# Router items moved in a layer-1 schedule, rows of their own for the last expert but one, and deviations of seven batches taken before the last residual

## What is computed

```
xn    = LN(x)                              # rows of x, over 128 channels
ao    = differential_attention(xn)         # per batch: softmax(q1 k1) - lam * softmax(q2 k2), 512 keys, times v, RMS norm
h     = LN1(xn); a = group_attention(h)    # over positions in a group, 16 heads
hid   = xn + a @ proj
r     = LN2(hid)                           # the rows that are routed
probs = softmax(r @ router)                # 8 experts, the best two per row, their weights made to sum to 1
for each expert e: out_e = gelu(rows_e @ w1_e) @ w2_e * weight     # up to 1280 rows each
moe   = scatter-add of out_e to the rows they came from
result = x + ao + hid + moe
```

## Time and profile before

| what | us |
|---|---|
| median of 3 runs (lowest, highest) | 1095.08 (1094.47, 1097.09) |
| the profiled execution | 1089.94 |
| its span | 1088.2 |
| PE busy | 921.2 (85%) |
| DVE busy | 712.0 (65%) |
| ACT busy | 624.8 (57%) |
| POOL busy | 567.9 (52%) |

### The profile page before, as it was taken

The page is one execution under the profiler, slowest core; times in us unless marked ns, Lnnn a source line. Parts: engine busy times, 40 slices in busy tenths (PEclk is TensorE's granted clock), DMA queues, the critical chain, the costliest instruction groups (busy, mean ns, idle before and its releaser), DMA issues.

```text
span 1088.2 us, 20697 instructions
## 1 busy us (share of the span) xinstructions
PE 921.2 (85%) x6587; PEld 616.8 (57%) x6624; DVE 712.0 (65%) x1511; ACT 624.8 (57%) x1127; POOL 567.9 (52%) x643
## 2 busy tenths in 40 slices
PE   7688879988999899899999868677888886999890
PEld 4366654477555455555555445444555655998880
DVE  6788852125777677677766565999857773646356
ACT  6566654512878687687878646344578653333320
POOL 3300029270675576566742217998306771788772
PEclk9899989999999999999999969988899997999995
DMA  5011121343101011101101059500011102222229
GB/s 144 1 78 77 77 79 58 136 139 123 31 21 31 19 23 24 28 20 28 24 21 30 2 92 188 178 1 0 6 34 43 50 26 80 83 78 90 75 75 269
DMA packets 75567, 70.23 MB, mean 65 GB/s; under 512 B 6706, under 2 KB 68604, under 8 KB 73440
## 3 DMA queue, kind: packets, MB, share of 16 engines
q1 hardware_dynamic: 65120, 59.84, 20.0%
q0 software_dynamic: 4608, 6.64, 1.8%
q10 hardware_dynamic: 5760, 2.70, 0.9%
HBM read 32.04 MB, written 31.60 MB: 58 GB/s over the span
## 4 chain that ended last, share of the span: by engine, by line
PE 33%; DVE 17%; POOL 9%; issue 9%; ACT 2%; DMA 2%; SPq 1%; DVEq 0%; ACTq 0%; POOLq 0%
PE banks L1984 6%; PE banks L1956 5%; PE banks L1970 5%; POOL y_dram L975 4%; PE banks L2010 4%; DVE B_mneg L1150 2%; PE banks L1958 2%; PE banks L2119 2%; DVE D_dmx L1256 2%; PE banks L2023 2%; PE banks L2068 1%; DVE banks L1305 1%; DVE D_sc L1282 1%; POOL rows_dram L930 1%; SPq L729 1%
## 5 line engine op out<-in xcount | busy, mean ns | idle before, releaser
L1150 DVE TENSOR_REDUCE B_mneg<-banks 128x2 f32<-128x256 f32 (+3 forms) x256 | 208.5, 824 | 78.1 <-PE banks L1958 69.5
L1623 ACT ACTIVATE B_pt<-banks 128x1024 f32<-128x1024 f32 (+3 forms) x256 | 178.7, 708 | 73.9 <-PE banks L1970 68.9
L791 POOL TENSOR_SCALAR_AFFINE_SELECT B_pt<-B_pt 128x512 f32<-128x512 f32 x128 | 81.2, 635 | 171.6 <-ACT B_pt L1623 162.5
L1956 PE MATMUL banks<-B_kp,B_qt 128*128 128x128 bf16 (+3 forms) x507 | 124.9, 300 | 1.8 <-DVE B_mneg L1150 0.6
L1970 PE MATMUL banks<-B_qt,B_kp 128*128 128x256 bf16 (+3 forms) x480 | 105.4, 297 | 12.0 <-issue 5.1
L1958 PE MATMUL banks<-B_mask_q,B_identb 128*128 128x128 bf16 x512 | 102.0, 219 | 0.7 <-issue 0.6
L1772 ACT ACTIVATE F_gh<-banks 128x512 f32<-128x512 f32 (+1 forms) x96 | 50.0, 527 | 82.8 <-PE banks L2188 78.3
L1984 PE MATMUL banks<-B_pt,B_vp 128*32 128x512 f32 (+3 forms) x1024 | 95.9, 446 | 1.5 <-ACT B_ot L1629 0.7
L930 POOL DMA_INDIRECT rows_dram<-F_xs,F_rowi x64 | 62.5, 976 | 61.7 <-DVE F_xs L1343 42.8
L975 POOL DMA_INDIRECT y_dram<-F_yo,F_ide x70 | 70.9, 1012 | 41.7 <-issue 19.2
L2119 PE MATMUL banks<-D_qk 128*128 128x512 f32 x128 | 75.2, 673 | 11.6 <-DVE D_pr L1267 11.6
(11 more groups left out here) (288 smaller groups left out, 2182.4 us busy)
## 6 DMA issues: line engine op xcount, KB each, us to landing
comb_dram<-C_comb SPq DMA_DIRECT2D x8, 1024.0 KB, 3.9
C_cst<-comb_dram SPq DMA_DIRECT2D x8, 1024.0 KB, 4.8
B_kp<-B_kt SPq DMA_DIRECT2D x64, 128.0 KB, 2.4
rows_dram<-D_zeros SPq DMA_DIRECT2D x8, 650.0 KB, 15.0
F_xe<-rows_dram SPq DMA_DIRECT2D x8, 650.0 KB, 3.9
C_w<-w_in SPq DMA_DIRECT2D x16, 256.0 KB, 2.9
y_dram<-D_zeros SPq DMA_DIRECT2D x2, 2048.0 KB, 16.8
F_gw<-mw_in SPq DMA_DIRECT2D x16, 256.0 KB, 3.0
```

The source lines that it names most:

```text
L791: g.affine_select(out=w, in_=w, compare_op=ALU.is_ge, fill=0.0, base=0, pattern=[[0, G], [1, P]], channel_multiplier=-1).then_inc(B_md, 1)
L1150: v.tensor_reduce(mneg[:, g % 2, qt, 2 * hp:2 * hp + 2], banks2[pair_of_banks(item)][:, :, 0:(qt + 1) * P], X, ALU.max, negate=True).then_ ...
L1623: a.activation(pt[:, 2 * hp:2 * hp + 2, PT_AT[kt]:PT_AT[kt] + w], banks2[pair_of_banks(item)][:, :, 0:w], ACT.Exp).then_inc(B_ex, 1)
L1956: t_.matmul(dst, qt1[:, g % 2, hp, qt * P:(qt + 1) * P], kp[:, g % NG, hp, h, 0:(qt + 1) * P], start=True, stop=False)
```

## The change

Three parts.

1. **Router table.** S gets the time 144.7 instead of 152.7. The pairs start at 147.3 + 18.0h instead of 155.3 + 14.1h: 147.3, 165.3, 183.3 and 201.3 instead of 155.3, 169.4, 183.5 and 197.6. All router items move with their pair.
2. **Deviations.** The deviations of the first seven batches are taken before the residual of the last batch, those of the last batch between the first three `norm_rows`. ACT's four roots stand ahead of its wait for the end of layer 0, and ahead of its first copy of turned rows.
3. **The tail.** Expert 6 gets rows of its own, `y_last_but_one`, as expert 7 has `y_last`: one more zero fill of 2 MB, and the two folding instructions for expert 6 too. SP loads `y_dram` when experts 0 to 5 have been scattered, then `y_last_but_one` in 4 pieces. The last iteration of the expert loop is written out on PE and DVE, without the items of a next pair. In it DVE adds `y_dram` for five batches before expert 7's first `yo`, and for three after its last. `y_last` is loaded into the place of `od`, without waiting for adds.

The diff, without the renamed semaphores, the new place of `rst2` and `var2`, and the arguments of the PE round:

```diff
--- before.py
+++ after.py
@@ -305,9 +305,9 @@
         yield t0 + 30.7, ("h", k, 0)
-    yield 152.7, ("S", 0, 0)
+    yield 144.7, ("S", 0, 0)
     for h in range(B // 2):
-        t0 = 155.3 + 14.1 * h
+        t0 = 147.3 + 18.0 * h
         for q in (2 * h, 2 * h + 1):
...
@@ -684,8 +685,9 @@
                              zeros[:, 0:D].unsqueeze(1).broadcast_to([P, TILES, D])).then_inc(D_z, 16)
-            sp.dma_start(y_last[:, :].rearrange("(p n) d -> p n d", p=P),
-                         zeros[:, 0:D].unsqueeze(1).broadcast_to([P, TILES, D])).then_inc(D_z, 16)
+            for k in range(2):
+                sp.dma_start(y_late[k][:, :].rearrange("(p n) d -> p n d", p=P),
+                             zeros[:, 0:D].unsqueeze(1).broadcast_to([P, TILES, D])).then_inc(D_z, 16)
@@ -717,17 +719,16 @@
-            sp.wait_ge(G_x[0], 16 * (EXP // 2))
-            sp.sem_inc(G_x[0], 16)
-            sp.wait_ge(G_w[0], 32 * (EXP // 2))
-            sp.sem_inc(G_w[0], 32)
-
             for par in range(2):
-                sp.wait_ge(G_zs[par], 16 * CT * (EXP // 2 - par))
+                sp.wait_ge(G_zs[par], 16 * CT * (EXP // 2 - 1))
             for b in range(B):
                 for k in range(2):
                     sp.dma_start(xs[:, b, k, :, 0:D], y_dram[(k * B + b) * T:(k * B + b + 1) * T, :].rearrange(
-                        "(t p) d -> p t d", p=P)).then_inc(G_bk[b], 16)
+                        "(t p) d -> p t d", p=P)).then_inc(G_bk[b // 2], 16)
+            sp.wait_ge(G_zs[0], 16 * CT * (EXP // 2))
+            for c in range(B // 2):
+                sp.dma_start(y[:, 2 * c * NT:(2 * c + 2) * NT, :], y_late[0][2 * c * T:(2 * c + 2) * T, :].rearrange(
+                    "(t p) d -> p t d", p=P)).then_inc(G_bs[c], 16)
             for b in range(B):
@@ -864,7 +865,6 @@
-            pool.wait_ge(D_sd, 1)
             own.link(g.memset(zeros[:], 0.0))
...
@@ -932,7 +932,7 @@
-            pool.wait_ge(D_sd, 2)
+            pool.wait_ge(D_sd, 4)
             for kind, a_, n in D_PLAN.order:
@@ -965,16 +965,16 @@
                 pool.wait_ge(G_id, e + 1)
-                last = e == EXP - 1
-                if last:
+                late = e - (EXP - 2)
+                if late >= 0:
                     own.link(g.tensor_scalar(second[:], ide[:, par, :], B * T, B * T, ALU.is_ge, ALU.mult))
                     own.link(g.tensor_tensor(ide[:, par, :], ide[:, par, :], second[:], ALU.subtract))
                 for c, (n0, n) in enumerate(CHUNKS):
                     pool.wait_ge(G_ys, G_ROUNDS.passed("y", pr, False, "y", par, c))
                     for m in range(n0, n0 + n):
                         pool.indirect_dma_start(
-                            out=(y_last if last else y_dram)[:, :], out_offset=bass.IndirectOffsetOnAxis(ap=ide[:, par, m:m + 1], axis=0),
-                            in_=yo[:, par, m, :], in_offset=None, bounds_check=(1 if last else 2) * B * T - 1, oob_is_err=False
+                            out=(y_late[late] if late >= 0 else y_dram)[:, :], out_offset=bass.IndirectOffsetOnAxis(ap=ide[:, par, m:m + 1], axis=0),
+                            in_=yo[:, par, m, :], in_offset=None, bounds_check=(1 if late >= 0 else 2) * B * T - 1, oob_is_err=False
                         ).then_inc(G_zs[par], 16)
@@ -1171,12 +1171,14 @@
-                def residual(g):
+                def residual(g, stats=True):
                     dve.wait_ge(B_mf, B_ROUNDS.passed("misc", it, False, "W", g, 0))
                     dve.wait_ge(B_bo, at(it, g // NG, 1, 1))
                     xb = x[:, bass.ds(it * (2 * NT) + (g // NG) * NT, NT), :].rearrange("p t d -> p (t d)")
                     own.link(v.tensor_tensor(xb, bank[6][:], xb, ALU.add))
                     dve.sem_inc(B_me, 1)
+                    if not stats:
+                        return
@@ -1202,8 +1204,30 @@
                         normalise(g)
+                    elif kind == "W" and last and g == PG - 1:
+                        deviations_of(FIRST_BATCHES, 1)
+                        residual(g, stats=False)
                     elif kind == "W":
                         residual(g)
+
+
+            FIRST_BATCHES, LAST_BATCH = slice(0, TILES - NT), slice(TILES - NT, TILES)
+
+            def variances_of(tiles):
+                v.tensor_copy(sd[:, tiles], st[:, tiles, 1]).then_inc(D_var, 1)
+
+            def deviations_of(tiles, n):
+                if tiles == FIRST_BATCHES:
+                    variances_of(tiles)
+                dve.wait_ge(D_sd, n)
+                own.link(v.reciprocal(rstd[:, tiles], sd[:, tiles]))
+                own.link(v.tensor_tensor(var2[:, tiles], rstd[:, tiles], rstd[:, tiles], ALU.mult))
+                v.tensor_tensor(var2[:, tiles], var2[:, tiles], st[:, tiles, 1], ALU.mult).then_inc(D_var, 1)
+
+            def second_deviations_of(tiles, n):
+                dve.wait_ge(D_sd, n)
+                own.link(v.reciprocal(rst2[:, tiles], var2[:, tiles]))
+
             dve_round(-1, True)
@@ -1213,15 +1237,17 @@
-            v.tensor_copy(sd[:], st[:, 0:TILES, 1]).then_inc(D_var, 1)
-            dve.wait_ge(D_sd, 1)
-            own.link(v.reciprocal(rstd[:], sd[:]))
             dve.wait_ge(B_end, 5)
-
-            own.link(v.tensor_tensor(var2[:], rstd[:], rstd[:], ALU.mult))
-            v.tensor_tensor(var2[:], var2[:], st[:, 0:TILES, 1], ALU.mult).then_inc(D_var, 1)
-            dve.wait_ge(D_sd, 2)
-            own.link(v.reciprocal(rst2[:], var2[:]))
+            second_deviations_of(FIRST_BATCHES, 2)
+
+            def last_batch_stats():
+                for t in range(NT):
+                    ins = v.bn_stats(bn6[:, t, :], x[:, TILES - NT + t, :])
+                own.link(ins)
+                for t in range(NT):
+                    ins = v.bn_aggr(st[:, TILES - NT + t, :], bn6[:, t, :])
+                own.link(ins)
+                variances_of(LAST_BATCH)
@@ -1397,6 +1423,12 @@
                     norm_rows(a_)
+                    if a_ == 0:
+                        last_batch_stats()
+                    elif a_ == 1:
+                        deviations_of(LAST_BATCH, 3)
+                    elif a_ == 2:
+                        second_deviations_of(LAST_BATCH, 4)
                 elif kind == "lam" and a_ != 1:
@@ -1432,11 +1464,22 @@
-            def dve_round_g(it, first):
+            def rows_of(b):
+                return slice(b * NT, (b + 1) * NT)
+
+            def add_earlier(b):
+
+                dve.wait_ge(G_bk[b // 2], 64)
+                own.link(v.tensor_tensor(x[:, rows_of(b), :], x[:, rows_of(b), :], xs[:, b, 0, :, 0:D], ALU.add))
+                own.link(v.tensor_tensor(x[:, rows_of(b), :], x[:, rows_of(b), :], xs[:, b, 1, :, 0:D], ALU.add))
+
+            BESIDE_LAST = 5
+
+            def dve_round_g(it, first, last=False):
                 skips = {"t": Skip(G_ROUNDS, dve, G_ts, "t"), "y": Skip(G_ROUNDS, dve, G_ys, "y")} if first else None
                 for item in G_ROUNDS.order:
                     kind, e, c = item
-                    if kind == "h" or (first and item not in G_ROUNDS.early):
+                    if kind == "h" or (first and item not in G_ROUNDS.early) or (last and item in G_ROUNDS.early):
                         continue
@@ -1469,23 +1512,26 @@
                         skips[kind].after(item)
+                    if last and item == ("t", 1, 2):
+                        dve.wait_ge(F_xo, 1)
+                        for b in range(BESIDE_LAST):
+                            add_earlier(b)
             dve_round_g(-1, True)
-            with dve.Fori(0, EXP // 2) as it:
+            with dve.Fori(0, EXP // 2 - 1) as it:
                 own.loop(it, 2 * (2 * 3 + 2))
                 dve_round_g(it, False)
-            own.end_loop(EXP // 2)
-
-            dve.wait_ge(F_xo, 1)
+            own.end_loop(EXP // 2 - 1)
+            dve_round_g(EXP // 2 - 1, False, True)
+
+            for b in range(BESIDE_LAST, B):
+                add_earlier(b)
             for b in range(B):
-                dve.wait_ge(G_bk[b], 32)
-                xb = x[:, b * NT:(b + 1) * NT, :]
-                own.link(v.tensor_tensor(xb, xb, xs[:, b, 0, :, 0:D], ALU.add))
-                v.tensor_tensor(xb, xb, xs[:, b, 1, :, 0:D], ALU.add).then_inc(G_xe, 1)
+                dve.wait_ge(G_bs[b // 2], 16)
+                ins = v.tensor_tensor(x[:, rows_of(b), :], x[:, rows_of(b), :], y[:, rows_of(b), :], ALU.add)
+            own.link(ins)
             for b in range(B):
-                dve.wait_ge(G_xe, b + 1)
                 dve.wait_ge(G_bl[b], 16)
-                xb = x[:, b * NT:(b + 1) * NT, :]
-                v.tensor_tensor(xb, xb, xs[:, b, 0, :, 0:D], ALU.add).then_inc(G_xr, 1)
+                v.tensor_tensor(x[:, rows_of(b), :], x[:, rows_of(b), :], od[:, rows_of(b), :], ALU.add).then_inc(G_xr, 1)
@@ -1651,12 +1697,13 @@
             act.sem_inc(B_end, 1)
+            a.activation(root[:], eps[:], ACT.Sqrt)
```

(13 more changed lines are left out.)

20 lines of the change are left out of this document (11 added, 9 removed).

## The result

| | before | changed |
|---|---|---|
| median, us | 1095.01 (4 runs, 1094.47 to 1097.09) | 1106.66 (4 runs, 1104.05 to 1109.96) |
| ratio, 95% interval | | 1.0112 (1.009 to 1.0134) |
| profiled execution, its span, us | 1089.94, 1088.2 | 1105.35, 1103.6 |
| mean granted clock | 0.945 | 0.940 |

The change makes the kernel 11.65 us slower. The forecast was +5.3, to 1100.4, with a range up to 1106.5. The sign is right, the size is 2.2 times the forecast, and the time lies 0.2 above the range.

A forecast was written before the change was run, and what follows sets the result against it. POOL's scatters from the first pair on and the pace of the pairs were taken to bound layer 1's end, nearly together. Table +6.4, deviations 0, tail -1.1: +5.3 on 1095.08 gave 1100.4, range 1088.0 to 1106.5.

The forecast's parts named there:

- The walk: Router table: four engines stepped through the new order with measured durations; pair 3's places at 892.3, scatters' end +10.9 us.
- pace: Router table: pairs follow at the old rate per table unit; pair 3 5.3 us later, at 883.4, scatters' end +2.0.
- the middle between pace and walk: Router table's term: +6.4 us, between +2.0 and +10.9, since later pairs have slack and late items are partly caught up.
- The low bound: Router table: pair 3 behind one more `s` and `c`, ready at 879.9 instead of 878.13; scatters' end -1.5 us.
- Part 2, deviations: Start of layer 1: waiting for ACT's fourth root replaces the wait removed; 0 us, bounds -3.0 and +0.5.
- term (e): Tail, last scatter's end to first load: `y_dram` loads run some 17 us earlier and no longer crowd it; -1.4 us.
- term (c): Tail, expert 7's scatters: splits for a pair that does not exist go, adds beside later scatters stay; -0.8 us.
- (d): Tail: ten adds beside expert 6's scatters lengthen them; +0.4 us, up to +6.9 by the skill page's exclusion rule.
- Term (b): Tail: two folding steps for expert 6 on POOL, which is full there; +0.68 us.
- attention absorbs the moved items: Rival, router table: moved items fill room on DVE and ACT, no change; 1092.5 to 1096, chance 0.26.
- the first scatter decides: Rival, router table: POOL starts 6.0 us earlier and never waits; 1088.0, chance 0.21 for faster.
- The walk in full: Rival, router table: all of +10.9 less 1.1, giving 1104.9; far end of the forecast's case, within slower's 0.53.

The follow-up runs named there:

- pair0_ahead: Kernel before with the deviations and only router pair 0 (with S) moved ahead by 8.0, pairs 1 to 3 unchanged: 1097.19 us against 1093.57, ratio 1.0042.
- pair3_back: Kernel before with only pair 3 of the router table moved back by 3.7: 1098.27 us against 1093.57, ratio 1.0055.
- adds_after: As old_table_again, but no adds beside expert 6's scatters, all sixteen behind expert 7's last result: 1169.26 us against 1170.73, ratio 0.9992, with stalls.
- old_table_again: Kernel before with deviations and tail changed, old router table kept: 1170.07 us against 1170.73, ratio 1.0020, with stalls.
- places_behind_c: Kernel before with the new router table alone, pair 0's places one attention difference later: 1103.64 us against 1093.57, ratio 1.0110.

## Why the prediction was right and wrong

**Part 1, first pair: right.** `r` of pair 0 was forecast 6.0 us earlier, and is 6.3 from the mark. The first scatter was said to start at 814.7 and did at 813.06 - 0.9 = 812.2 on the clock of the trace before (0.9 is how much later the mark is in the changed kernel's trace).

**The walk: right within 2.7 us, and on the low side.** It gave 811.4, 840.7 and 892.3 for `r` of pairs 0, 1 and 3, and +10.9 for the scatters' end. On that clock they are at 811.1, 843.4 and 894.7, and the scatters end 13.4 later. The step from pair 1 to pair 3 was forecast with 51.6 us at the old pace, and took 895.60 - 844.21 = 51.4.

**The step that failed: "I take the middle between pace and walk, +6.4".** The reason given was that later pairs have slack and a late item is partly caught up. The runs show no catching up: the last scatter ends 13.4 us later than before from the mark, 2.5 beyond the far end, and another 0.9 are lost in the landing and load behind it (923.01 - 915.62 = 7.4 us against 6.45). The loss grows from pair to pair instead, 6.6, 10.6 and 16.6 us. The table's term was put at +6.4, and the stretch measured +14.3 in the profiles. With the walk's +10.9 in the sum the forecast would have been 1104.9. Averaging a worked-out value with one that knew nothing of the order was the error. The walk itself missed 2.7 us at pair 1: 0.7 of them were there when ACT began its rows (820.31 - 0.9 = 819.4, and 818.8 said), and 2.0 came after. The likely place of these is that PE now turns the rows of pair 1 ahead of the product which DVE's output waits for, which the prediction does not name. pair0_ahead, where they are turned behind it, fits with its 2 us at that output, but no run tried this by itself without stalls.

The slack of the pairs was also counted too large: "4.5 early" and "4.1 early" leave out the 0.84 us from DVE to POOL that the prediction uses elsewhere, so they were 3.7 and 3.3.

**The low bound, one more `s` and one more `c` at 0.60 and 1.16: too low.** pair3_back makes exactly this move. Its `r` of pair 3 began at 882.45, 97.5 us from its mark, against 873.40 - 782.56 = 90.8 before: 6.6 us for two DVE steps of 1.8 together (6.1 if the 0.5 already lost at pair 2 is left out). Ahead of it, from 871 us on, DVE waited 2.66 and 0.91 us for PE's score products and 1.49 for an ACT exponential (L1695). The pace (5.3 us) was nearer.

**Part 2, deviations: right.** PE's first product of layer 1 comes sooner, ACT's first copy does not:

```profile
643.80 0.30 ACT L1705 ACTIVATE var<-var,eps 128x4 f32<-128x4 f32 x1 [1.92 <-DVE var L1225]
644.01 1.43 ACT L1716 ACTIVATE D_lyT<-banks,D_lnc 128x512 f32<-128x512 f32 x2
...
634.18 2.08 PE L2067 MATMUL banks<-wo,B_aT 128*128 128x128 f32 x8 [0.67 <-ACT B_aT L1660]
640.30 1.09 PE L2109 MATMUL banks<-ident,D_ly 128*128 128x128 f32 x4 [4.04 <-DVE D_ly L1266]
```

ACT's fourth root is at 643.80, the copy at 644.01. From the last residual's product, 634.18, this is 9.8 us, and before it was 642.78 - 632.75 = 10.0. The product L2109 starts 6.1 us behind it instead of 8.9. The 2.7 us are gained and lost again at ACT, and the forecast of 0 holds without stalls, by the profiles of the changed kernel.

**Part 3, tail: term (e) right, term (c) of the wrong sign; -1.1 forecast and +0.2 measured.** POOL's and ACT's queue's rows of the last two experts:

```profile
1055.55 1.06 POOL L975 DMA_INDIRECT y_last_but_one<-F_yo,F_ide  x1 [0.78 <-POOL F_ide L971]
...
1068.04 1.43 POOL L975 DMA_INDIRECT y_last_but_one<-F_yo,F_ide  x1 [0.30 <-issue]
...
1071.48 1.08 POOL L975 DMA_INDIRECT y_last<-F_yo,F_ide  x1 [1.01 <-DVE F_yo L1510]
...
1079.92 1.50 POOL L975 DMA_INDIRECT y_last<-F_yo,F_ide  x1 [0.30 <-issue]
1081.73 1.34 POOL L975 DMA_INDIRECT y_last<-F_yo,F_ide  x1 [0.30 <-issue]
...
1084.65 0.97 POOL L975 DMA_INDIRECT y_last<-F_yo,F_ide  x1 [0.30 <-issue]
...
1086.90 3.18 ACTq L1826 DMA_DIRECT2D D_od<-y_last  x6
```

Term (e) was -1.4: from the last scatter's start to the end of the span are 18.95 us instead of 20.7, -1.8. Terms (c) and (d) were -0.4 together and are +1.7: from expert 6's first scatter to expert 7's last 29.1 us instead of 27.4. Of these 0.7 come from the adds beside expert 6 (12.5 us for nine pitches instead of 11.8), 0.5 from the change of experts, and expert 7's nine pitches did not gain 0.8 but lost 0.5, since adds of `y_last_but_one` lie beside scatters of 1.50 and 1.34 us. Term (b), the folding for expert 6, lies ahead of this: 1.85 us from POOL's step before it (L951) to expert 6's first scatter instead of 0.93, +0.9 where +0.7 was said. From the experts' first product to that scatter it is all the same only 0.3 us longer, so the experts ahead gave 0.6 back. The adds did not block expert 7: the fifth batch's waited 1.59 us for its load, but its first `yo` waited for POOL (1.32), not the reverse.

Ten adds held by a whole instruction each were to cost up to 6.9 us. The rows show 0.18 us a scatter (adds_after against old_table_again), and not an add's 0.69; beside expert 6 in the changed kernel (d) is 0.7, and 0.4 was said. The Trainium skill, "SBUF — State Buffer", section "SBUF: two separate sides", says that the later of the two instructions blocks until the first is done: the step in which adds and scatters run fits this in kind, and so do the folding steps that take 0.3 to 0.4 us longer beside adds. The size does not follow from it as I had priced it, since scatters lose what is missing to two adds, 0.17 us, and not an add each.

**The rivals.** That attention absorbs the moved items and that the first scatter decides are both refuted by pair0_ahead. The walk in full, named as the far end at 1104.9, is what happened, and 1.8 us more.

## What to carry to other kernels

When an item is moved ahead in an in-order schedule, look on every engine at what stands behind it, above all at work for which a third engine waits; on a stretch where engines wait for each other in turn, a step can cost far more than its own time (6.6 us here for 1.8 us of DVE). The wait moves where the pace is set: POOL's start 8.5 us earlier from the mark was worth nothing, since the pairs behind it set the end. And where an order has been walked through with measured durations, take its number, and widen the range instead of pulling the value toward the hope.

## What the runs showed of the hardware

- A scatter issued by POOL takes 0.97 us, 1.15 beside a VectorE add of two SBUF operands, and 1.34 to 1.50 beside some of the later adds; its pitch becomes that of two adds, 1.45 instead of 1.28 us. Small POOL steps on 128x10 take 0.57 to 0.67 us beside such adds, and 0.20 to 0.28 without (old_table_again, adds_after).
- In 14 of 18 experiments engines stood idle without a reason in the trace, ACT up to 16 us at once. The same kernel then takes 1165 to 1171 us instead of 1094 to 1095, and small effects change size: the table costs 0.55 to 1.04% there; without stalls it costs 1.10% in places_behind_c, and with the other two parts 1.12 and 1.26%. What the stalls are is open.
- A score product of two matmuls took 1.12 us behind an idle time of 0.30 us and 2.08 behind 4.59, and the two after it 1.92 and 1.76 for products that take 1.05 and 1.02 otherwise.
